# The sync engine sends the shift first in a step of layer 0's attention, then the loads of the stacks, then the store

## What is computed

```python
# q and k with rotary embedding, 16 heads of 16; k, v from the context
offsets = jnp.arange(-W, 1)[None, :]          # W = 64
idx = q_pos + offsets
local_mask = (idx < 0) | (idx >= S_k)
scores = jnp.einsum('bhqd,bhqwd->bhqw', q, k_win)
scores = jnp.where(mask, -jnp.inf, scores)
m = jnp.max(scores, axis=-1, keepdims=True)
e = jnp.exp(scores - m)
denom = jnp.sum(e, axis=-1, keepdims=True)
probs = jnp.where(denom > 0, e / jnp.where(denom > 0, denom, 1.0), 0.0)
ctx = jnp.einsum('bhqw,bhqwd->bhqd', probs, v_win)
```

## Time and profile before

| | |
|---|---|
| median of 3 runs (lowest, highest) | 6424.18 us (6423.8, 6430.1) |
| the profiled execution: time, span | 6420.89 us, 6419.1 us |
| PE, DVE, ACT, POOL busy over the span | 81%, 50%, 39%, 16% |
| the stage of the 64 steps | from 503.56 to about 1202 us of the span |
| granted TensorE clock, mean of the span | 0.895 of full speed |

### The profile page before, as it was taken

One profiled execution on the slowest core, in us unless ns is written; L12 is line 12 of the kernel. 1 busy time (PEld: TensorE's weight loads), 2 busy tenths in 40 slices (PEclk: granted clock), 3 DMA queues, 4 the chain that ended last, 5 costly groups with the idle time before them and its releaser, 6 DMA issues. The chain is left out here.

```text
span 6419.1 us, 90576 instructions
## 1 busy us (share of the span) xinstructions
PE 5200.6 (81%) x27631; PEld 2744.0 (43%) x27632; DVE 3186.6 (50%) x6296; ACT 2506.3 (39%) x3173; POOL 1019.4 (16%) x786
## 2 busy tenths in 40 slices
PE   6767777678955999999999999999976059999970
PEld 3434444453422444444444444444435036666650
DVE  4544444331133788787878787878844100000013
ACT  1223333211111477676767676767641011211210
POOL 3430000130133000000000000000014520000016
PEclk8888888899977899999999999999977579999995
DMA  6443333471046533333333333333326331211115
GB/s 214 118 116 108 108 109 105 137 227 44 26 132 173 77 65 65 61 64 56 64 59 64 62 65 65 65 65 65 49 68 207 113 100 47 68 50 50 54 54 182
DMA packets 384125, 580.78 MB, mean 90 GB/s; under 512 B 85304, under 2 KB 279287, under 8 KB 381584
## 3 DMA queue, kind: packets, MB, share of 16 engines
q1 hardware_dynamic: 369008, 525.77, 34.2%
q0 software_dynamic: 14768, 50.51, 2.2%
HBM read 299.26 MB, written 197.24 MB: 77 GB/s over the span
## 5 line engine op out<-in xcount | busy, mean ns | idle before, releaser
L1152 DVE TENSOR_REDUCE full_peak<-full_item 128x1 f32<-128x512 f32 (+2 forms) x3392 | 2038.0, 655 | 500.5 <-PE full_item L1219 494.3
L1122 ACT ACTIVATE full_prob<-full_score 128x1024 f32<-128x1024 f32 (+1 forms) x1792 | 1651.4, 961 | 675.3 <-PE full_score L1230 668.1
L1219 PE MATMUL full_item<-full_kst,full_qst 49*128 49x512 f32 (+1 forms) x4096 | 1210.1, 408 | 43.6 <-DVE full_peak L1152 23.8
L1230 PE MATMUL full_score<-full_qst,full_kst 51*128 51x512 f32 (+1 forms) x3328 | 1116.4, 450 | 37.0 <-issue 24.3
L1230 PEld LDWEIGHTS full_score<-full_qst,full_kst 51*128 51x128 f32 (+1 forms) x3328 | 483.6, 184 | 956.5 <-ACT full_prob L1122 605.6
L1244 PE MATMUL full_value<-full_prob,full_vaug 128*17 128x512 f32 x6656 | 890.6, 607 | 0.5 <-ACT full_raw L1109 0.3
L1219 PEld LDWEIGHTS full_item<-full_kst,full_qst 49*128 49x128 f32 x4096 | 634.5, 190 | 188.1 <-DVE full_peak L1152 128.7
L2041 ACT ACTIVATE moe_hT<-moe_hbank,moe_b 128x512 f32<-128x512 f32 (+1 forms) x320 | 199.4, 623 | 801.6 <-PE moe_hbank L2096 797.2
L2108 PE MATMUL moe_ybank<-moe_w,moe_hT 128*128 128x256 f32 x2176 | 485.8, 384 | 5.2 <-ACT moe_hT L2041 5.2
L2096 PE MATMUL moe_hbank<-moe_xT,moe_w 128*128 128x512 f32 (+1 forms) x1280 | 477.2, 531 | 6.2 <-DMA moe_b<-in_b 6.0
L2108 PEld LDWEIGHTS moe_ybank<-moe_w,moe_hT 128*128 128x128 f32 x2176 | 414.9, 192 | 67.6 <-issue 6.0
(11 more groups left out here) (207 smaller groups left out, 5401.5 us busy)
## 6 DMA issues: line engine op xcount, KB each, us to landing
full_kst<-full_high SPq DMA_DIRECT2D x256, 200.1 KB
full_ctxT<-in_ctxT SPq DMA_DIRECT2D x17, 1601.0 KB
full_kst<-full_low SPq DMA_DIRECT2D x128, 200.1 KB
full_qst<-scratch_q SPq DMA_DIRECT2D x384, 64.0 KB
scratch_xbuf<-ctxp_zero POOLq DMA_DIRECT2D x17, 1024.0 KB
scratch_attn<-win_raw SPq DMA_DIRECT2D x64, 256.0 KB, 2.3
scratch_q<-open_parts SPq DMA_DIRECT2D x128, 128.0 KB, 2.3
scratch_attn<-full_raw SPq DMA_DIRECT2D x64, 256.0 KB, 2.1
```

Source lines behind the costliest of these rows:

```text
L1122: nc.scalar.activation(prob[h][(s.par * PAIRS + t) % 2][0:rows, 0:banks, :], score[u % 2][0:rows, 0:banks, :], ACT.Exp, scale=SCALE).then_ ...
L1152: nc.vector.tensor_reduce(peak[s.par][:, hq:hq + len(qts), c], src, AX, ALU.max).then_inc(item_read, 1)
L1219: ins = nc.tensor.matmul(ps[:, at:at + z - a], qst[s.slot][rows, h // 2, qt * P:(qt + 1) * P].bitcast(F32R), kst[s.slot][rows, h // 2, a:z ...
L1230: ins = nc.tensor.matmul(score[u % 2][0:z - a, kt % 2, :], kst[s.slot][rows, h // 2, a:z].bitcast(F32R), qst[s.slot][rows, h // 2, :].bitc ...
```

## The change

In a step, SP used to issue the loads of the step three ahead, then the shift of the next step, then the store of the step before. Now it issues the shift, then the loads, then the store. Nothing is added or taken away: same transfers, same waits, same buffers.

```diff
             def window(s, first, left):
+                if left >= 1:
+                    send_shift(s.plus(1))
                 if first or not isinstance(s.n, int) or s.n + 3 < STEPS:
                     if not first:

                         sp.wait_ge(score_full, UNITS * s.n)
                         sp.wait_ge(vaug_done, s.n)
                     load(s.plus(3))
-                if left >= 1:
-                    send_shift(s.plus(1))
                 if not first:
                     store(s.plus(-1))
             windows(sp, window)
```

## The result

The changed kernel takes 6700.27 us (median of three, 6699.94 to 6711.53) where the kernel before takes 6424.18 us: slower by 4.35%, with a 95% interval of the ratio of 1.0421 to 1.045. The profiled execution took 6699.94 us, with a span of 6698.1 us, 279.0 us more than the span before.

What follows compares the result with a forecast made beforehand. PE waits for the shift queued behind loads (181.7 us at line 778); moved, the loads bind. Steps of 1.15 + 11.5 + 3.95 = 16.6 us, sixty of them, cost 337 us: 6761 us, range 6685 to 6815, opened to 6650 to 6820.

Steps and rivals of the forecast that it cites:

- next late thing: The loads at line 762's first max item: 14.36 us from start to need, against about 12 us taken.
- Term a: On SP, from the shift's issue to the first load's: 1.15 us, bounds 0.85 and 1.15.
- Term b: From the first load's issue until PE can go on: 11.5 us taken, 8.5 below and 12.35 above.
- The row of 11.16 us: Start of the stage: loads from 509.58, PE released at 520.74; claimed that nothing was issued over their tail.
- first rival: Tail of the loads shrinks when nothing runs over it; first load to PE's go 8.5 to 10.5 us; chance 0.10.
- Term c: From window's first max item to next shift's issue: 3.95 us, at 1.2 GHz because of the wait ahead.
- The sum: Over the stage: first item at 518.75 plus 60 x 16.6 gives 1514.75, against 1179.57; 337 us lost with the clock.
- the ring: Closed loop per step, shift's issue through loads and first max item to next shift: 16.6 us in place of 10.96.
- Hidden anyway, faster: At windows' first max items, loads cause no lateness; only the shift's waits vanish, down to 6242 us; chance 0.04.
- turning point: First load to PE's go of 7.45 us at full clock; below that the kernel gains.
- A ring near today's 11 us: Skill's bandwidth rule for the loads: 896 KB in about 5.4 us, some 7.4 with issue and receipt costs.
- No change, bound by the two engines: Two DMA engines of the loads' tail are the bound, the queue's order indifferent; no change; chance 0.03.

Runs made afterwards that it cites:

- e3: Changed kernel with the store issued ahead of the loads (shift, store, loads): 6963.57 us, 1.0829 to 1.0865 of the kernel before.
- e2: Changed kernel with q's three transfers replaced by six of 16 rows: 6365.74 us, 0.9899 to 0.9932 of the kernel before.
- e5: Kernel before, its order kept (loads, shift, store), with q in six transfers of 16 rows: 6201.82 us, 0.9633 to 0.9673 of the kernel before.
- e7: Changed kernel with 384 KB of k read once more behind each store into an unused buffer: 6747.02 us, 1.0492 to 1.0527 of the kernel before.
- e1: Changed kernel with only q's first transfer (48 rows) split into three of 16 rows: 6594.22 us, 1.0249 to 1.0284 of the kernel before.
- e4: Kernel before with the shift issued by GpSimd, not SyncE, the loads still early: 6380.15 us, 0.9926 to 0.9961 of the kernel before.

## Why the prediction was right, point by point

**Where the next late thing is.** The prediction said that the shift is what PE feels today and the loads are the next late thing, with some 2.4 us to spare. Shown: 61 waits at line 762, 384.6 us in all or 6.3 us each (forecast: some 60 of about 7 us, 430 us), and 8.3 us left at line 778. e3 raised the dose and the step followed; e2 against e5 showed that it is the order that costs, with the loads of either length.

**Term a**, shift to first load: 1.15 us predicted, 1.13 us measured in the mean. Right.

**Term b**, first load to PE's go: 11.5 us predicted, 10.73 us measured in the mean of 61 rings. This is the term that was mis-sized, and 60 x 0.77 = 46 us of the sum are this term. The row of 11.16 us, which the prediction took as the nearest, was misread. It says that nothing was issued over the tail of the loads from 509.58. But PE was released at 520.74, and SP's timeline of the kernel before has ahead of that:

```profile
517.75 0.39 SPq L647 DMA_DIRECT2D scratch_attn<-win_raw  x1
518.25 1.28 SPq L630 DMA_DIRECT2D win_kst<-scratch_k  x3
```

A store and the next loads ran over the last 3 us there too, and all these rows of before ended with the landing of the shift, not of the loads. At the same place of the changed kernel the first load is issued at 507.11 and PE goes on at 517.51, 10.40 us. e7 shows that transfers behind a load lengthen it, by 0.87 us for 384 KB. In the kernel before a store of 256 KB and the next loads, 896 KB, were issued there, in the changed kernel the store alone, and before the mean from first load to PE's go was 11.94 us in the 30 windows that waited behind their loads, 1.2 us more than in the changed kernel. How these 1.2 us divide between the traffic and the shift's own passage behind the loads was not tested, and stays open. The prediction had named the traffic as its first rival, but dismissed it by the misread row, and added 0.34 us to that row in place of taking any off. The rival's mechanism was thus real; its size, b between 8.5 and 10.5 us, was not reached.

**Term c**, first max item to next shift: 3.95 us predicted, 3.96 us in the mean. Right, and so was its reason, the clock at its lower level behind the wait. e2 shows the other side, 2.35 us at full clock.

**The sum.** The prediction had window 61's item at 1514.75 and a loss of 337 us; it started at 1467.44, 287.9 us later than before, where 335 were forecast. The span grew by 279.0 us, 9 us less than that: behind this item the changed program took 5230.7 us and the one before 5239.5. That is within the scatter of this long remainder (5221 to 5240 us in the profiles of all nine kernels), and "nothing behind the stage changes" holds up to it. 6700 against 6761 us: the forecast's own range of 6685 to 6815 held. Its low end doesn't follow from its terms, though: with b at 10.5 and c at 3.4 us the ring is 15.05 and not 15.3 us, which is about 6668 us.

**The rivals.** *Hidden anyway, faster*: wrong for these loads, but its turning point agrees with e2. The prediction put it at b = 7.45 us; e2 has 6.7 us and is 0.8% faster than the kernel before (0.9899 to 0.9932), in the changed order. A ring near today's 11 us, which the prediction also weighed, did not come with these loads of 10.73 us; e2 has it, with loads of 6.7 us and a ring of 10.39 us. *No change, bound by the two engines*: out, the DMA share is 0.00 from 818 to 822, and e3's step of 20 us could not have been. That the tail comes from the copies of q was argued, from the share of 0.12 above all; e1 and e2 have now shown it. The removed waits were counted as "up to 181.7 us", and they did vanish; they never stood in the sum, and rightly, since the new wait covers them.

**What it did not see.** It took the shift's late landing for a matter of SP's queue. e4 showed that a queue of its own leaves 119.5 of the 181.7 us, and e5 that without the tail the same place in the queue costs 2.4 us and not 7.6. This had no bearing on its number.

## What to carry to other kernels

A queue's order has two ends: before moving a small urgent transfer ahead of a large early one, look up when the large one is needed and how long it takes, not how many steps "ahead" it is called. If the moved wait and the landing close a ring through the compute engine, its length is the sum of the parts and every step pays it. And where a load shows a long tail on two DMA engines, mend the transfer's shape first; here that was worth more than the order: 0.965 of the time in the old order, where the new order alone gave 1.0435.

## What the runs showed of the hardware

- A load of 896 KB took about 10.7 us with q's 48 and 32 rows read as copies, and 6.7 us with the same bytes in transfers of 16 rows, with three more issues.
- A transfer of 12 KB alone on GpSimd's queue took 6.3 us in the mean to PE's go while loads with a tail ran on SP's (e4). On SP's queue behind such loads it took 7.6 us, and behind loads without a tail 2.4 us (e5).
- 384 KB issued behind a load on the same queue lengthened it by 0.87 us (e7).
- In a wait of 7.39 us the clock had fallen within the wait, and behind it PE ran at 1.2 GHz for the next 4 us. In e2 a wait of 2.91 us left it at its upper level and one of 2.87 us did not.
